# The expert stage of a routed vision-transformer layer, from chunks of 1024 rows against one weight set to chunks of two 512-row units side by side

## The chip, the cores and the metric

The kernel runs on one core of a Trainium2 chip. The metric is the device time of one execution in microseconds (us), here the median of three runs. Beside them stands one more execution, taken with the hardware profiler; all views of the profile are of that execution.

## The reference

Thirty-two images of 1024 patches each are embedded into 64 features. A single-head attention with layer norm follows, and then the part that matters here, a layer of 8 experts with top-1 routing:

```python
C = ceil(1.25 * T / E)                       # T = 32768 tokens, E = 8, C = 5120 slots per expert
idx = argmax(softmax(x @ gate_w + gate_b)); prb = its probability
pos = place of the token among those of its expert; kept = pos < C
hmid = relu(buf[e] @ w1[e] + b1[e])          # 64 -> 256
ybuf = hmid @ w2[e] + b2[e]                  # 256 -> 64
y = nan_to_num(ybuf[idx, pos] * (prb * kept), nan=0, posinf=1e4, neginf=-1e4)
out = layernorm(h + y)
```

All data are fp32. The output is 32 x 1024 rows of 64 numbers.

## The kernel before

The kernel has two stages that follow each other. The first runs over 32 windows, one image each: projections, attention, layer norm and gate, with the instructions of several images interleaved by hand (`run_windows`). GpSimd ends each window by scattering the 1024 rows into a DRAM tensor `slots` of 8 x 5120 rows by an indirect DMA each for 128 rows (L1052). A row has 66 numbers: 64 features, the probability and the token's number. None of this is touched by the change.

The second, the expert stage, begins when the last of those scatters has landed (the waits ahead of the first `load_chunk` on SyncE). It runs over 40 chunks of 1024 slots, 5 for each expert. Every engine has its own program, written out in order, and they meet only in semaphores. For chunk c:

- SyncE loads the chunk's rows into `b_in` (L368), a ring of 5 buffers (`NIN`). Each partition gets 8 rows that follow each other. The load for chunk c + 5 waits until chunk c has been normalized (`b_o_ready`). The weights of an expert have 2 buffers.
- TensorE turns the rows: 8 transposes into `p_st` (L546). Then come `hidden` (L555), which multiplies 65 rows (64 features and a row of ones that brings the bias) with `w1` in fp32, 4 products of 512 columns in 8 records, and the second product (L571): 16 products of 64 columns in 32 records, with the hidden values stationary and `w2` moving, so that the result already has tokens on partitions. It goes to one of two halves of `p_misc`. The order of the program is hidden(c), turn(c + 1), second product(c).
- ScalarE copies the turned rows out (`b_xT`, L664), applies Relu to the two halves of the hidden layer (L681, 1024 columns each), and computes squares and square root for the layer norm two chunks behind (L668, L672). In the first chunks this lag is one instead of two.
- VectorE adds `b2` (L908), makes three masks (L940, L941, L946) and replaces NaN, plus and minus infinity by three predicated copies (L927), multiplies by the probability (L932), adds the residual (L937), and normalizes (L944 to L971). The token numbers become integers in `b_ix` (L962). Before it writes `b_ix` and `b_o` of a ring place, it waits until the scatter that reads the place has landed. The steps of chunk c and of chunk c + 1 alternate in its program. For the first two chunks the tail of a chunk is issued at once, without the alternation (`if first and m < 2`).
- GpSimd waits for `b_o_ready` and issues 8 indirect DMAs of 128 rows, which scatter `b_o` to the output by `b_ix` (L1084).

Ahead of the stage TensorE runs 12 + 1 products that nobody reads (`keep_warm`). The loops are hardware loops over pairs of experts (`run_pairs`). A wait with a computed value goes through a register (`wait_apart`).

## Time and profile before

| | |
|---|---|
| Times of three runs | 1368.55, 1369.12, 1375.61 us |
| Median | 1369.12 us |
| The profiled execution | 1370.71 us |
| Its span in the profile | 1368.9 us, mean granted TensorE clock 0.933 of full speed |
| Busy: TensorE, VectorE, ScalarE, GpSimd | 1218.2, 941.1, 579.4, 884.0 us |
| First rows of the expert stage loaded from | 899.8 us |
| Output scatters (320) | 925.1 us to 1364.0 us |

A busy share is the mean over both stages, which have different limits, so the views that follow are cut to the expert stage. In all views PE is TensorE's products, PEld its weight loads, DVE VectorE, ACT ScalarE, POOL GpSimd and SP SyncE. L and a number is a line of the kernel. An fp32 product shows as two records, one of type fp32r as one. A granted clock of 1.00 is 2.4 GHz, one of 0.50 is 1.2 GHz.

### The profile page before, as it was taken

To read this page: it belongs to the slowest core of one execution; us is meant where nothing else is said; L and a number is where in the kernel's file an instruction comes from. 1 tells how busy PE (TensorE), PEld (TensorE's weight loads), DVE (VectorE), ACT (ScalarE), POOL (GpSimd) and SP (SyncE) were. 2 spreads that over 40 slices of the span, in tenths; PEclk is the share of its full clock that TensorE was granted. 3 is DMA by queue.
4 is the path that set the end of the run, shared out by engine and by line. 5 is a ranking of instruction groups with operands and counts; after the bars stand their busy time and mean duration, and the time that the engine had idled before them with its cause. 6 is when DMAs were issued, how large, how long until landed. Compare 5 with 4: busy or idle time off the path is not lost.

```text
span 1368.9 us, 21037 instructions
## 1 busy us (share of the span) xinstructions
PE 1218.2 (89%) x6088; PEld 770.6 (56%) x6088; DVE 941.1 (69%) x1766; ACT 579.4 (42%) x746; POOL 884.0 (65%) x950
## 2 busy tenths in 40 slices
PE   3999999999999999999999999599999999899600
PEld 2565666566565565656566555256667676666400
DVE  5577777777776777767777766329999777677610
ACT  1354455455554555545555544224444433333200
POOL 1137667657656666756766765737777777777776
PEclk9999999999999999999999999799999977969655
DMA  7843343333344234234334330011112111011000
GB/s 227 277 118 89 99 104 88 83 90 95 73 99 95 67 96 99 72 85 97 86 85 97 79 74 18 19 48 35 39 38 54 47 30 41 21 38 25 1 2 0
DMA packets 53485, 100.23 MB, mean 73 GB/s; under 512 B 22970, under 2 KB 25223, under 8 KB 53382
## 3 DMA queue, kind: packets, MB, share of 16 engines
q1 hardware_dynamic: 32646, 84.32, 24.9%
q0 software_dynamic: 20736, 14.62, 3.8%
q8 instruction: 54, 0.88, 0.3%
q14 instruction: 49, 0.40, 0.1%
HBM read 25.58 MB, written 38.34 MB: 47 GB/s over the span
## 4 chain that ended last, share of the span: by engine, by line
PE 66%; POOL 18%; issue 8%; DVE 3%; ACT 2%; DMA 2%; POOLq 1%; SPq 0%; DVEq 0%; ACTq 0%
PE p_u L478 17%; POOL out L1084 16%; PE p_st L462 10%; PE p_sm L448 9%; PE p_st L465 8%; PE p_misc L571 4%; PE p_misc L436 4%; PE p_misc L491 4%; PE p_misc L421 3%; PE p_sm L555 2%; PE p_u L555 2%; ACT b_h L681 1%; POOL slots L1052 1%; ACT pT L623 1%; DMA out<-b_o,b_ix 1%
## 5 line engine op out<-in xcount | busy, mean ns | idle before, releaser
L1052 POOL DMA_INDIRECT slots<-rows,idx x256 | 274.8, 1073 | 249.5 <-DVE acc L869 142.2
L782 DVE TENSOR_REDUCE mx<-p_sm 128x1 f32<-128x1024 f32 x252 | 308.3, 1224 | 166.9 <-PE p_sm L448 166.2
L1084 POOL DMA_INDIRECT out<-b_o,b_ix x320 | 341.7, 1068 | 119.9 <-issue 96.0
L623 ACT ACTIVATE pT<-p_st 128x1024 f32<-128x1024 f32 x256 | 262.3, 1024 | 266.7 <-PE p_st L465 265.3
L478 PE MATMUL p_u<-pT,vv 128*64 128x512 f32 x1024 | 261.8, 611 | 0.0
L462 PE MATMUL p_st<-mQ,sK 128*128 128x512 f32 x512 | 178.5, 430 | 6.4 <-ACT pT L623 3.9
L448 PE MATMUL p_sm<-sK,mQ 128*128 128x512 f32 x504 | 169.8, 418 | 4.5 <-DMA sK<-lo 3.5
L571 PE MATMUL p_misc<-b_w,b_h 128*128 128x64 f32 x1280 | 163.7, 290 | 10.3 <-ACT b_h L681 10.3
L571 PEld LDWEIGHTS p_misc<-b_w,b_h 128*128 128x128 f32 x1280 | 159.7, 206 | 19.7 <-ACT b_h L681 18.2
L465 PE MATMUL p_st<-mR,sR 72*128 72x512 f32 x512 | 161.0, 395 | 0.0
L462 PEld LDWEIGHTS p_st<-mQ,sK 128*128 128x128 f32 x512 | 83.6, 189 | 96.3 <-ACT pT L623 59.7
L448 PEld LDWEIGHTS p_sm<-sK,mQ 128*128 128x128 f32 x504 | 88.6, 191 | 70.4 <-DVE mx L782 28.1
L478 PEld LDWEIGHTS p_u<-pT,vv 128*64 128x64 f32 x1024 | 56.4, 135 | 106.5 <-issue 106.5
L465 PEld LDWEIGHTS p_st<-mR,sR 72*128 72x128 f32 x512 | 96.8, 189 | 23.6
L555 PE MATMUL p_sm<-b_xT,b_w 65*128 65x512 f32 x160 | 86.6, 668 | 9.8 <-ACT b_xT L664 9.0
L555 PE MATMUL p_u<-b_xT,b_w 65*128 65x512 f32 x160 | 88.6, 683 | 0.0
L927 DVE COPY_PREDICATED b_y<-b_m,b_big 128x512 f32<-128x512 uint8 x120 | 87.7, 731 | 0.5
L681 ACT ACTIVATE b_h<-p_sm 128x1024 f32<-128x1024 f32 x40 | 40.9, 1021 | 100.3 <-PE p_sm L555 100.3
L601 ACT ACTIVATE hi<-p_misc 128x1024 fp32r<-128x1024 f32 x32 | 32.8, 1024 | 115.8 <-PE p_misc L421 115.8
L436 PEld LDWEIGHTS p_misc<-w_px,xt 114*128 114x128 f32 x512 | 70.9, 194 | 5.8
L436 PE MATMUL p_misc<-w_px,xt 114*128 114x137 f32 x512 | 72.1, 284 | 0.0
L491 PEld LDWEIGHTS p_misc<-w_j,uu 128*128 128x128 f32 x512 | 62.0, 192 | 5.0 <-ACT uu L628 2.4
(146 smaller groups left out, 1543.6 us busy)
## 6 DMA issues: line engine op xcount, KB each, us to landing
mQ<-hi SPq DMA_DIRECT2D x64, 256.0 KB, 3.9
slots<-init POOLq DMA_DIRECT2D x16, 660.0 KB, 7.4
b_in<-slots SPq DMA_DIRECT2D x40, 264.0 KB, 2.7
sK<-hi SPq DMA_DIRECT2D x32, 256.0 KB, 5.0
sK<-lo SPq DMA_DIRECT2D x32, 256.0 KB, 4.5
mR<-lo SPq DMA_DIRECT2D x32, 256.0 KB, 3.9
sR<-hi SPq DMA_DIRECT2D x32, 256.0 KB, 4.5
out<-o SPq DMA_DIRECT2D x32, 256.0 KB, 4.2
```

The source lines that it names most:

```text
L436: last = pe.matmul(p_misc[:, j // 2, (j % 2) * GP:(j % 2 + 1) * GP], xt[0:KTOK, p, t * P:(t + 1) * P], w_px[:, :], start=True, stop=True)
L448: last = pe.matmul(max_place(n, j)[:, a, :], mQ[t][:, j * P:(j + 1) * P], sK[t][:, a * HALF:(a + 1) * HALF], start=True, stop=True)
L462: pe.matmul(p_st[:, a, :], sK[t][:, k * P:(k + 1) * P], mQ[t][:, a * HALF:(a + 1) * HALF], start=True, stop=False)
L465: last = pe.matmul(p_st[:, a, :], sR[p][0:D + NT, k * P:(k + 1) * P], mR[p][0:D + NT, a * HALF:(a + 1) * HALF], start=False, stop=True)
L478: last = pe.matmul(p_u[c:c + D, a, :], vv[:, p, k, :], pT[k % 4][:, a * HALF:(a + 1) * HALF], start=(r == 0), stop=(r == 3))
L491: last = pe.matmul(p_misc[:, j // 4, (j % 4) * GT:(j % 4 + 1) * GT], uu[:, j * P:(j + 1) * P], w_j[:, :], start=True, stop=True)
L555: last = pe.matmul((p_sm, p_u)[f][:, a, :], b_w1[:, q, f * P:(f + 1) * P], b_xT[0:KA, a * HALF:(a + 1) * HALF], start=True, stop=True)
L571: mm = pe.matmul(p_y[m % 2][:, j, :], b_h[:, f, j * P:(j + 1) * P], b_w2[:, q, f, :], start=(f == 0), stop=(f == HB - 1))
L623: act.activation(pT[k % 4][:, :], flat(p_st), ACT.Exp).then_inc(exp_done, 1)
L782: dve.tensor_reduce(mx[:, p, j:j + 1], flat(max_place(n, j)), AX.X, ALU.max).then_inc(max_done, 1)
L1052: pool.indirect_dma_start(slots, bass.IndirectOffsetOnAxis(ap=idx[:, p, j:j + 1], axis=0), rows[:, p, j, :], None, bounds_check=SLOTS - 1, ...
L1084: pool.indirect_dma_start(out_rows, bass.IndirectOffsetOnAxis(ap=b_ix[:, m % NIN, j:j + 1], axis=0), b_o[:, m % NIN, j, :], None, bounds_c ...
```

## The change

The 1024 rows of a chunk are taken as two units of 512, u = 0 and u = 1, that lie side by side on partitions: 64 features of each.

- SyncE loads each chunk three times: `b_in` as before, and each unit's 64 features into the half of `b_x` that is its own. The ring has 4 places. A reload waits for `b_c_ready`.
- TensorE turns both units with 4 transposes of 128 x 128. The first product is split in three fp32r products (high x high, low x high, high x low), each once for the upper and once for the lower 64 rows of the array: 12 products of 512 columns. In the second product `w2` is stationary (64 columns) and the hidden values move: 4 fp32 products of 512 columns, the units going to the upper and lower 64 partitions of one bank. The result has features on partitions, so 4 more transposes turn it back. The program's order is hidden(c), down(c - 1), rows_turn(c + 1), turn_back(c - 1).
- ScalarE rounds the turned rows to the high part (512 columns), adds `b1` inside the Relu and `b2` inside a copy of the sums. The order is Relu 0 of c, root of c - 3, Relu 1 of c, sums of c - 1, high part of c + 1, squares of c - 2. A Relu waits until down(c - 1) is done, since `b_h` has one buffer.
- VectorE makes the low part from the high one, splits each expert's `w1`, and multiplies by the probability straight from the turned-back sums. NaN and infinities are replaced after that multiplication, by three `tensor_scalar`, one addition and one predicated copy. Residual and layer norm are as before. The order in step c is: low part of c + 1, weighing of c - 1, sum of squares of c - 2, replacement of c - 1, output of c - 2, residual and centring of c - 1.
- GpSimd does the same 320 scatters. All loops are written out. The first chunks have no order of their own any more.

```diff
-NIN = 5
+NC = E * NCH
+NIN = 4
+UNIT = CH // 2
+UT = UNIT // P
...
+            def load_expert(e):
+                q = e % 2
+                for h in range(2):
+                    sp.dma_start(b_w1[h * D:(h + 1) * D, q, :], w1[e, :, :]).then_inc(e_loaded[q], 16)
+                sp.dma_start(b_w2[:, q, :], w2[e, :, :]).then_inc(e_loaded[q], 16)
+            def load_chunk(c):
+                r = c % NIN
+                sp.dma_start(b_in[:, r, :, :].rearrange("p (u j) w -> p u (j w)", u=2), slots_c[c, :, :, :])\
+                    .then_inc(c_loaded[r], 16)
+                for u in range(2):
+                    sp.dma_start(b_x[:, r, :, u * D:(u + 1) * D], slots_x[c, :, u, :, :]).then_inc(c_loaded[r], 16)
...
+            for c in range(NC):
+                if c + NIN < NC:
+                    sp.wait_ge(b_c_ready, c + 1)
+                    load_chunk(c + NIN)
+                e = c // NCH + 2
+                if c % NCH == NCH - 1 and e < E:
+                    sp.wait_ge(b_y_done, c + 1)
+                    load_expert(e)
...
+            def rows_turn(c):
+                r = c % NIN
+                pe.wait_ge(c_loaded[r], 48 * (c // NIN) + 48)
+                if c >= 2:
+                    pe.wait_ge(b_tl_ready, c - 1)
+                for j in range(UT):
+                    last = pe.transpose(p_st[:, c % 2, j * P:(j + 1) * P], b_x[:, r, j, :], c_id[:, :])
                 last.then_inc(b_t_done, 1)
+            def hidden(c):
+                q, i = c // NCH % 2, c % 2
+                pe.wait_ge(b_w_ready, c // NCH + 1)
+                pe.wait_ge(b_tl_ready, c + 1)
+                for f, out in ((0, p_sm), (1, p_u)):
+                    if c >= 1:
+                        pe.wait_ge(b_relu, HB * (c - 1) + f + 1)
+                    cols = slice(f * P, (f + 1) * P)
+                    for w, t in ((b_w1h, b_th[i]), (b_w1l, b_th[i]), (b_w1h, b_tl[i])):
+                        for u in range(2):
+                            h = slice(u * D, (u + 1) * D)
+                            last = pe.matmul(out[:, u, :], w[h, q, cols], t[h, :],
+                                             start=(w is b_w1h and t is b_th[i]), stop=(t is b_tl[i]))
+                    last.then_inc(b_h_done, 1)
+            def down(c):
+                q = c // NCH % 2
+                pe.wait_ge(b_relu, HB * c + HB)
+                if c >= 1:
+                    pe.wait_ge(b_yT_ready, c)
                 for f in range(HB):
+                    for u in range(2):
+                        last = pe.matmul(p_y[u * D:(u + 1) * D, :], b_w2[:, q, f * D:(f + 1) * D],
+                                         b_h[:, f, u, :], start=(f == 0), stop=(f == HB - 1))
+                last.then_inc(b_y_done, 1)
+            def turn_back(c):
+                pe.wait_ge(b_yT_ready, c + 1)
+                if c >= 1:
+                    pe.wait_ge(b_p_ready, c)
+                for j in range(UT):
+                    last = pe.transpose(p_misc[:, 1, j * P:(j + 1) * P], b_yT[:, j * P:(j + 1) * P], c_id[:, :])
+                last.then_inc(b_back_done, 1)
...
+            for c in range(NC + 1):
+                if c < NC:
+                    hidden(c)
+                if c >= 1:
+                    down(c - 1)
+                if c + 1 < NC:
+                    rows_turn(c + 1)
+                if c >= 1:
+                    turn_back(c - 1)
...
+            def columns_high(c):
                 act.wait_ge(b_t_done, c + 1)
+                if c >= 2:
+                    act.wait_ge(b_h_done, HB * (c - 1))
+                act.activation(b_th[c % 2][:, :], p_st[:, c % 2, :], ACT.Copy).then_inc(b_th_ready, 1)
+            def rectify(c, f):
+                q = c // NCH % 2
+                act.wait_ge(b_h_done, HB * c + f + 1)
+                if c >= 1:
+                    act.wait_ge(b_y_done, c)
+                act.activation(b_h[:, f, :, :].rearrange("p u t -> p (u t)"), flat((p_sm, p_u)[f]), ACT.Relu,
+                               bias=b_w2[:, q, HB * D + f:HB * D + f + 1]).then_inc(b_relu, 1)
+            def sums_copy(c):
+                q = c // NCH % 2
+                act.wait_ge(b_y_done, c + 1)
+                if c >= 1:
+                    act.wait_ge(b_back_done, c)
+                act.activation(b_yT[:, :], p_y, ACT.Identity, bias=b_w2[:, q, HB * D + HB:HB * D + HB + 1])\
+                    .then_inc(b_yT_ready, 1)
             def squares(c):
                 act.wait_ge(b_c_ready, c + 1)
+                if c >= 1:
+                    act.wait_ge(b_vs_ready, c)
+                act.activation(b_sq[:, :, :], b_c[c % 2][:, :, :], ACT.Square).then_inc(b_sq_ready, 1)
             def deviation(c):
                 act.wait_ge(b_vs_ready, c + 1)
+                if c >= 1:
+                    act.wait_ge(b_rs_ready, c)
                 act.activation(b_sd[:, :], b_vs[:, :], ACT.Sqrt, bias=b_eps[:, 0:1], scale=1.0 / D)\
                     .then_inc(b_sd_ready, 1)
...
+            columns_high(0)
+            for c in range(NC + 3):
+                if c < NC:
+                    rectify(c, 0)
+                if 0 <= c - 3:
+                    deviation(c - 3)
+                if c < NC:
+                    rectify(c, 1)
+                if 0 <= c - 1 < NC:
+                    sums_copy(c - 1)
+                if c + 1 < NC:
+                    columns_high(c + 1)
+                if 0 <= c - 2 < NC:
+                    squares(c - 2)
...
+            def split_expert(e):
+                q = e % 2
+                dve.wait_ge(e_loaded[q], 48 * (e // 2) + 48)
+                if e >= 2:
+                    dve.wait_ge(b_y_done, NCH * (e - 1))
+                link(dve.tensor_copy(b_w1h[:, q, :], b_w1[:, q, :]))
+                dve.tensor_tensor(b_w1l[:, q, :], b_w1[:, q, :], b_w1h[:, q, :].bitcast(F32), ALU.subtract)\
+                    .then_inc(b_w_ready, 1)
+            def columns_low(c):
+                i = c % 2
+                dve.wait_ge(b_th_ready, c + 1)
+                if c >= 2:
+                    dve.wait_ge(b_h_done, HB * (c - 1))
+                dve.tensor_tensor(b_tl[i][:, :], p_st[:, i, :], b_th[i][:, :].bitcast(F32), ALU.subtract)\
+                    .then_inc(b_tl_ready, 1)
+            def rows_in(c):
+                return b_in[:, c % NIN, :, :]
+            def weigh(c):
+                dve.wait_ge(b_back_done, c + 1)
+                if c >= 1:
+                    dve.wait_ge(b_num_ready, c)
+                dve.tensor_tensor(b_p[:, :, :].rearrange("p (u j) d -> p u j d", u=2), p_back,
+                                  per_token(rows_in(c)[:, :, D], D).rearrange("p (u j) d -> p u j d", u=2), ALU.mult)\
+                    .then_inc(b_p_ready, 1)
+            def sum_of_squares(c):
+                dve.wait_ge(b_sq_ready, c + 1)
+                if c >= 1:
+                    dve.wait_ge(b_sd_ready, c)
+                dve.tensor_reduce(b_vs[:, :], b_sq[:, :, :], AX.X, ALU.add).then_inc(b_vs_ready, 1)
+            def to_numbers(c):
+                dve.wait_ge(b_p_ready, c + 1)
+                if c >= 1:
+                    dve.wait_ge(b_u_ready, c)
+                dve.tensor_scalar(b_fin[:, :, :], b_p[:, :, :], 0.0, 0.0, ALU.mult, ALU.is_equal)
+                dve.tensor_scalar(b_pos[:, :, :], b_p[:, :, :], 0.0, 1e4, ALU.max, ALU.min)
+                dve.tensor_scalar(b_neg[:, :, :], b_p[:, :, :], 0.0, -1e4, ALU.min, ALU.max)\
+                    .then_inc(b_clip_ready, 1)
+                dve.wait_ge(b_clip_ready, c + 1)
+                dve.tensor_tensor(b_n[:, :, :], b_pos[:, :, :], b_neg[:, :, :], ALU.add).then_inc(b_n_ready, 1)
+                dve.wait_ge(b_n_ready, c + 1)
+                dve.copy_predicated(b_n[:, :, :], b_fin[:, :, :], b_p[:, :, :]).then_inc(b_num_ready, 1)
+            def normalized(c):
+                r = c % NIN
+                dve.wait_ge(b_sd_ready, c + 1)
+                dve.reciprocal(b_rs[:, :], b_sd[:, :]).then_inc(b_rs_ready, 1)
+                dve.wait_ge(b_rs_ready, c + 1)
+                if c >= NIN:
+                    dve.wait_ge(b_scattered[r], 16 * NT * (c // NIN))
+                dve.tensor_tensor(b_o[:, r, :, :], b_c[c % 2][:, :, :], per_token(b_rs[:, :], D), ALU.mult)
+                dve.tensor_copy(b_ix[:, r, :], b_id[:, c % 2, :]).then_inc(b_o_ready, 1)
+            def centred(c):
+                dve.wait_ge(b_num_ready, c + 1)
+                dve.tensor_tensor(b_u[:, :, :], b_n[:, :, :], rows_in(c)[:, :, 0:D], ALU.add)\
+                    .then_inc(b_u_ready, 1)
+                dve.wait_ge(b_u_ready, c + 1)
+                dve.tensor_reduce(b_mu[:, :], b_u[:, :, :], AX.X, ALU.add).then_inc(b_mu_ready, 1)
+                dve.tensor_copy(b_id[:, c % 2, :], rows_in(c)[:, :, D + 1])
+                dve.wait_ge(b_mu_ready, c + 1)
+                dve.tensor_scalar(b_mm[:, :], b_mu[:, :], 1.0 / D, None, ALU.mult).then_inc(b_mm_ready, 1)
+                dve.wait_ge(b_mm_ready, c + 1)
+                if c >= 2:
+                    dve.wait_ge(b_o_ready, c - 1)
+                dve.tensor_tensor(b_c[c % 2][:, :, :], b_u[:, :, :], per_token(b_mm[:, :], D), ALU.subtract)\
+                    .then_inc(b_c_ready, 1)
+            split_expert(0)
+            columns_low(0)
+            for c in range(NC + 2):
+                if c + 1 < NC:
+                    columns_low(c + 1)
+                if 0 <= c - 1 < NC:
+                    weigh(c - 1)
+                if 0 <= c - 2:
+                    sum_of_squares(c - 2)
+                if 0 <= c - 1 < NC:
+                    to_numbers(c - 1)
+                if c % NCH == 2 and c // NCH + 1 < E:
+                    split_expert(c // NCH + 1)
+                if 0 <= c - 2:
+                    normalized(c - 2)
+                if 0 <= c - 1 < NC:
+                    centred(c - 1)
...
```

## Rows read from the trace of the kernel before

**Rows 1.** Chain that ended last, by engine and line, 1000 us to the end.

```profile
by line: POOL out L1084 59.4%; issue 17.6%; PE p_misc L571 7.1%; PE p_u L555 3.3%; PE p_sm L555 2.9%; DMA out<-b_o,b_ix 2.1%; ACT b_h L681 2.0%; POOLq L1084 1.5%; DVE b_y L927 0.7%; DVE b_o L971 0.6%; POOLq L51 0.3%; DVE b_vs L964 0.2%; DVE
```

**Rows 2.** The page's groups: shapes, count, busy us, mean ns, idle before and its releasers.

```profile
L1084 POOL DMA_INDIRECT out<-b_o,b_ix x320 | 341.7, 1068 | 119.9 <-issue 96.0 <-DVE b_o L971 24.0
```

**Rows 3.** Line 1084: durations ns least/median/greatest, start of the first and the last.

```profile
L1084 POOL DMA_INDIRECT out<-b_o,b_ix x320: 971/973/1501, 925.1 to 1363.0; - x160
```

**Rows 4.** Waits of VectorE from 903 us on: total us, times, longest.

```profile
DVE b_ix L962 <- DMA out<-b_o,b_ix: 67.5, 22, 5.8
```

**Rows 5.** Timeline of TensorE, one chunk (start, us, records, idle before and releaser).

```profile
1061.15 3.79 PE L571 MATMUL p_misc<-b_w,b_h 128*128 128x64 f32 x32 [0.24 <-ACT b_h L681]
1064.77 1.94 PE L555 MATMUL p_sm<-b_xT,b_w 65*128 65x512 f32 x4
1068.26 1.04 PE L546 MATMUL p_st<-c_wide,b_in 128*64 128x128 f32 x8
```

**Rows 6.** The same in a later chunk, behind a pause of TensorE.

```profile
1212.26 3.60 PE L555 MATMUL p_sm<-b_xT,b_w 65*128 65x512 f32 x4 [0.83 <-ACT b_xT L664]
```

**Rows 7.** Windows: busy us (records) by engine, then PEclk, DMA share, GB/s.

```profile
924.00:1092.00 168.00, 161.77 (x959) 117.16 (x958) 153.93 (x307) 74.31 (x97) 130.30 (x121) 1.00 0.17 43
1092.00:1290.00 198.00, 184.97 (x854) 129.21 (x852) 141.87 (x288) 67.51 (x89) 154.44 (x144) 0.79 0.12 27
```

**Rows 8.** Timeline of TensorE in the attention stage: column halves, then fp32r products.

```profile
508.11 1.94 PE L478 MATMUL p_u<-pT,vv 128*64 128x512 f32 x8
...
510.37 0.71 PE L421 MATMUL p_misc<-xh,w_qkh 114*128 114x512 f32 x2
...
511.86 0.63 PE L462 MATMUL p_st<-mQ,sK 128*128 128x512 f32 x2
```

**Rows 9.** Groups by shape of VectorE and ScalarE, 903 us on, columns as rows 2.

```profile
L927 DVE COPY_PREDICATED b_y<-b_m,b_big 128x512 f32<-128x512 uint8 x120 | 87.7, 731 | 0.5
...
L681 ACT ACTIVATE b_h<-p_sm 128x1024 f32<-128x1024 f32 x40 | 40.9, 1021 | 100.3 <-PE p_sm L555 100.3
...
L971 DVE TENSOR_TENSOR b_o<-b_c,b_rs 128x512 f32<-128x512 f32 x40 | 28.0, 701 | 2.8
L908 DVE TENSOR_TENSOR b_y<-p_misc,b_b 128x512 f32<-128x512 f32 x40 | 27.5, 687 | 32.1 <-PE p_misc L571 30.1 <-issue 1.9
...
L940 DVE TENSOR_SCALAR b_m<-b_y 128x512 uint8<-128x512 f32 x40 | 17.0, 424 | 0.1
...
L672 ACT ACTIVATE b_sd<-b_vs,b_eps 128x8 f32<-128x8 f32 x40 | 11.8, 295 | 60.1 <-DVE b_vs L964 60.1
L949 DVE TENSOR_SCALAR b_mm<-b_mu 128x8 f32<-128x8 f32 x40 | 9.6, 240 | 0.1
...
L969 DVE RECIPROCAL b_rs<-b_sd 128x8 f32<-128x8 f32 x40 | 7.6, 190 | 1.7 <-ACT b_sd L672 1.7
```

**Rows 10.** Timeline at the start of the expert stage, SyncE and TensorE.

```profile
899.76 2.23 SPq L368 DMA_DIRECT2D b_in<-slots  x5
...
902.52 1.06 PE L546 MATMUL p_st<-c_wide,b_in 128*64 128x128 f32 x8 [2.22 <-DMA b_in<-slots]
```

**Rows 11.** Timeline: first square root, first output, first scatter.

```profile
921.69 1.28 ACT L672 ACT_TABLE_LOAD   x1
...
923.55 0.69 DVE L971 TENSOR_TENSOR b_o<-b_c,b_rs 128x512 f32<-128x512 f32 x1
...
925.14 1.11 POOL L1084 DMA_INDIRECT out<-b_o,b_ix  x1 [22.75 <-DVE b_o L971]
```

**Rows 12.** Timeline: two scatters beside VectorE.

```profile
1114.82 0.68 DVE L964 TENSOR_REDUCE b_vs<-b_sq 128x8 f32<-128x512 f32 x1
1115.11 0.97 POOL L1084 DMA_INDIRECT out<-b_o,b_ix  x1 [0.30 <-issue]
...
1116.33 0.69 DVE L971 TENSOR_TENSOR b_o<-b_c,b_rs 128x512 f32<-128x512 f32 x1
1116.39 1.48 POOL L1084 DMA_INDIRECT out<-b_o,b_ix  x1 [0.30 <-issue]
```

239 lines of the change are left out of this document (51 added, 188 removed).

## The prediction

> **What bounds the kernel now.** I read the chain of waits first, because the two stages have different limits and a busy share over both says little. From 1000 us to the end, which lies wholly in the expert stage, the chain is made of output scatters and the "issue" gaps between them [rows 1]. The reader is to see there that TensorE's products come in only in the first 50 us. The group of the scatters gives the price: 320 of 1.068 us each, 341.7 us, with 96.0 us of gaps of 0.30 us [rows 2]. The first starts at 925.1 us and the last at 1363.0 us [rows 3]. So GpSimd runs without a pause for 438.9 us, or 8 x 1.368 = 10.94 us for a chunk. The waits of VectorE say the same from the other side: 67.5 us for scatters to land, in order to get a ring place back [rows 4]. TensorE needs 1.77 + 1.71 + 1.28 + 3.62 = 8.4 us for a chunk at full clock, the distance between the starts of its pieces [rows 5], so it runs ahead until the ring is full.
>
> **The sum's frame.** The profiled execution took 1370.71 us, its span is 1368.9, so 1.8 us lie outside; it stands 1.6 us above the median of 1369.12. The last scatter ends at 1364.0, 4.9 us before the span's end. A change in this stage can move the time by three things only: when the first scatter starts, what a scatter costs, and whether a chunk is ready every 10.94 us.
>
> **The scatter itself** isn't changed. Its least duration is 0.971 us and its mean 1.068 [rows 2, 3]; the rest is 0.097 x 320 = 31 us. The timeline shows what makes it. A scatter that starts in the middle of a reduction takes 0.97. One that starts at 1116.39, 0.06 us into the output multiplication, takes 1.48, and what it has in excess is about what was left of that instruction [rows 12]. I take it that a scatter waits for VectorE instructions with two SBUF inputs, and for the fast `tensor_scalar` (0.42 us for 512 elements, where an addition takes 0.69) [rows 9]. Per chunk there were 5 of the first kind, 3 predicated copies of 0.73 and 2 `tensor_scalar`; now there are 4, 1 and 3. If the excess goes by the square of their durations, it falls from 4.3 to 3.0 units, or 31 us to about 22: a gain of 9 us. Bounds: 31 us of gain, none, or 10 us of loss, if the phases meet badly.
>
> The Trainium skill has this rule in "SBUF — State Buffer", "Who interferes with whom": the second port pair of VectorE is shared with GpSimd and held for a whole instruction by operations with two SBUF inputs or in a two-port mode. By it the gain is real as far as those instructions become fewer, and the trace agrees with its 1.48 against 0.97.
>
> **The work of a chunk now, first on TensorE.**
> - Hidden: 12 fp32r products of 512 columns. Six of them one after the other took 1.49 us (510.37 to 511.86) [rows 8], so 3.0 us if the two units exclude each other, 1.5 if they run fully side by side. What is nearest is the pair of column halves in the attention stage: 8 fp32 records in 1.9 us [rows 8], where 4 records of the same width take 1.77 in a row [rows 5]; about 0.24 instead of 0.44 each. I take 1.8.
> - Down: 4 fp32 products, 8 records, of exactly that form: 1.94 us; 3.5 if in a row.
> - Eight transposes of 128 x 128: 8 of half the width took 1.04 [rows 5], so 0.5 to 1.1 for each group of 4; I take 0.7. They lie beside ScalarE's work.
>
> TensorE thus falls from 8.4 to about 5.2 us at 2.4 GHz. By itself that is worth nothing, since it waited already.
>
> "TensorEngine Tiling", "Key Properties", in the Trainium skill says that tiles run in parallel and that a change of the tiling mode drains the engine. Hidden, down and the transposes are three modes. No row here shows row tiles; the column halves agree with the first part. By that part alone hidden would take 1.5 us and a chunk 9.0; for the drains neither the page nor a row has a price.
>
> **The loop.** The new orders close a ring through four engines. hidden(c + 1) needs the low part of c + 1, which VectorE makes only after centring c - 2. That stands behind output(c - 3), which waits for the root on ScalarE. The root is queued behind Relu 0 of c, and this Relu waits for down(c - 1), behind hidden(c) on TensorE. So in each chunk these follow each other with nothing beside them:
> - low part of the next chunk 0.69, as the addition that reads 512 elements from PSUM [rows 9], and 0.08 to TensorE;
> - hidden and down 1.8 + 1.94 = 3.74;
> - Relu 1.02 and root 0.30 [rows 9], 0.09 for two hand-overs;
> - reciprocal 0.19, output 0.61, numbers to `b_ix` 0.20, 0.04 of hand-over;
> - residual 0.68, row sum 0.68 [rows 12], scaling 0.24, centring 0.60, three hand-overs of 0.04: 2.32.
>
> Sum: 0.77 + 3.74 + 1.41 + 1.04 + 2.32 = 9.28 us. Weighing, replacement (3 x 0.42, 0.69, 0.73) and the sum of squares, 4.0 us, lie beside hidden, down, Relu and root, 5.1 us; the split of `w1`, 0.6 us on every fifth chunk, fits in barely. Behind the Relu's added wait stand the sums copy and the high part, and for them wait turn_back and VectorE.
>
> 9.28 us would still be under 10.94. But TensorE now works in one burst of 3.7 us and two small groups of transposes, and pauses for 4 us in each chunk, five times the 0.83 us behind which it fell to 1.2 GHz. At 1.2 GHz hidden and down take 7.5 us, and they lie on the ring: 13.0 us for a chunk. At that pace TensorE is mostly busy and should rise again, as it did in rows 7's second window. There the mean of 0.79 means 0.42 of the time at the lower clock, with TensorE busy in 185 of 198 us. With more pauses I take 0.6: 9.28 + 0.6 x 3.74 = 11.5 us. The bounds are 9.3 and 13.0.
>
> **The start.** The first chunk's order of its own is gone. Before, from the first load issue at 899.76 [rows 10] to the first scatter at 925.14 [rows 11] there were 25.4 us. Now the load is three pieces, two of them in runs of 256 bytes: 904.5 instead of 902.5 (one load took 2.7 us, the added pieces cost 0.5 to 4; I take 2). Turn, high and low part 0.7 + 0.6 + 0.7: 906.5. The low part of chunk 1 follows hidden, two Relus and a high part: 911. From there to the low parts of chunks 2 and 3 it is 3.74 + 2 x 1.02 + 0.6 + 0.6 + 0.7 + 0.3 = 8.0 us each: 927. Then hidden(3) and down(2) 3.74, Relu 1.02, table load 1.28 [rows 11], root 0.30, output 1.1: 934.5. At 1.2 GHz throughout some 13 us more, 948. I take 941. The first scatter starts 0.9 us after its rows, as before (923.55 + 0.69 to 925.14) [rows 11].
>
> **The loads.** 40 x 3 instead of 40, issued four chunks ahead; at 11 us a chunk a landing of 5 or even 10 us is hidden. The ring of 4 instead of 5 holds 4 x 10.94 = 44 us of scatters. It costs nothing while VectorE is at most three chunks ahead. Without that cover each scatter's landing would be on the chain. The second load of weights now waits for down; it has five chunks of time. Written-out loops: nothing, bounds -1 to +2.
>
> **The sum.** 941 + 39 x 11.53 (449.7) + 0.9 + the last 8 scatters, beside an idle VectorE, 9.9 + 4.9 + 1.8 = 1408 us, 38 above the profiled execution.
>
> **Rivals.**
> - The scatters stay the bound. If the clock holds, or 9.3 us are right nearly throughout: 934.5 + 0.9 + 438.9 - 9 + 4.9 + 1.8 = 1372 us. For it speaks the margin of 1.6 us per chunk and the full clock up to 1092 us; against it the pauses. 0.24.
> - Always 1.2 GHz, or row tiles that exclude each other (which gives 10.5 us and 15.5 us): 948 + 39 x 13.0 + 17.5 = 1473 us. For it: 4 us of pause. Against: the clock came back several times between 1092 and 1290. 0.13.
> - Faster: fewer instructions on VectorE give GpSimd its 0.97 us, at 10.2 us a chunk. This decides if the ring runs below 10.2 us and less than half of the 31 us stays. 934.5 + 0.9 + 438.9 - 31 + 6.7 = 1350, with half of it 1366; middle 1358. For it: two predicated copies fewer. Against: four two-input operations stay and the start loses 9 us. 0.13.
>
> **How the numbers follow.** The forecast has 0.50, with a range of its own of 1384 to 1440 (0.4 to 0.8 of the time at the lower clock, or other starts). The range for 8 in 10 takes in the scatter-bound case and stops inside the two outer ones: 1363 to 1464. 0.5% is 6.8 us, so faster is below 1362.3 and slower above 1376.0; this is about what a measurement of this kernel can tell. The scatter-bound case divides into 0.03 faster, 0.14 same and 0.07 slower, the faster rival into 0.12 and 0.01 same. So faster is 0.15, same 0.15, slower 0.07 + 0.50 + 0.13 = 0.70.
>
> **What would show it.** The first output scatter at 935 to 948 us. Scatters with pauses in front of them put down to VectorE's output, over 100 us in all, where they were 1.3 besides the first. A distance of 11 to 12 us between the Relus of successive chunks. A granted clock near 0.7 in the stage, with hidden taking 1.8 us in some chunks and 3.6 in others. A mean scatter of 1.00 to 1.05 us. VectorE waiting for the root, no longer for scatters to land. It is wrong if GpSimd's pauses stay under 5 us, if hidden takes 3 us at full clock, or if the clock is 1.00 in spite of the pauses.

## The result: slower by 1.6%, and the profile after

The changed kernel took 1395.1 us in the median of four runs (1390.5 to 1398.0), the kernel before 1369.7 beside it. The ratio is 1.0159, with an interval of 1.0124 to 1.0193. The profiled execution took 1398.0, span 1396.2. Forecast were 1408 and "slower"; the mechanism behind that number was not the one that came.

First the page's row of the output scatters, their line, and the waits from 903 us on (us, times, longest), which answer to [rows 2], [rows 3] and [rows 4].

```profile
L1130 POOL DMA_INDIRECT out<-b_o,b_ix x320 | 350.4, 1095 | 136.9 <-issue 93.0
...
L1130 POOL DMA_INDIRECT out<-b_o,b_ix x320: 970/974/1507, 944.6 to 1392.3; - x160
...
DVE b_rs L992 <- ACT b_sd L725: 98.6, 38, 4.6
POOL out L1130 <- issue: 93.0, 305, 0.3
POOL out L1130 <- DVE b_ix L997: 44.0, 15, 38.7
DVE b_o L996 <- DMA out<-b_o,b_ix: 14.5, 6, 5.5
```

VectorE now waits for the root, 98.6 us, as forecast. But GpSimd waited for rows only 44.0 - 38.7 = 5.3 us besides the first time, where the forecast names over 100 as its sign. So the scatters still set the pace, and they became dearer: 1095 ns in place of 1068. The end is the first scatter's start, the scatters, the gaps between them, pauses, and what follows the last:

| us | start | scatters | gaps | pauses | tail | span |
|---|---|---|---|---|---|---|
| before | 925.1 | 341.7 | 96.0 | 1.3 | 4.9 | 1368.9 |
| after | 944.6 | 350.4 | 93.0 | 5.3 | 2.9 | 1396.2 |
| difference | +19.5 | +8.7 | -3.0 | +4.0 | -2.0 | +27.3 |

The first load was issued 3.5 us later than before. The way from there to the first scatter is 15.9 us longer, which is the largest part of the loss.

The windows (columns as in [rows 7]) show the clock: lower at once, where it had been 1.00 to 1092 us. The third and fourth are two pieces of one round of 10.24 us.

```profile
945.00:1030.00 85.00, 52.23 (x226) 27.46 (x224) 61.44 (x131) 32.02 (x48) 65.71 (x61) 0.79 0.25 54
1030.00:1230.00 200.00, 118.72 (x546) 65.53 (x548) 151.87 (x324) 76.70 (x115) 158.21 (x138) 0.83 0.29 66
...
1041.50:1044.90 3.40, 2.96 (x14) 2.07 (x16) 3.37 (x7) 0.40 (x1) 2.68 (x3) 0.50 0.68 155
1044.90:1051.80 6.90, 3.13 (x16) 1.26 (x16) 4.92 (x13) 3.66 (x6) 5.48 (x5) 0.99 0.02 1
```

The timeline of one chunk, with only the rows on the ring and the scatters beside them, shows both the ring and why a scatter is dear.

```profile
1037.66 0.29 ACT L725 ACTIVATE b_sd<-b_vs,b_eps 128x8 f32<-128x8 f32 x1
...
1037.93 0.97 POOL L1130 DMA_INDIRECT out<-b_o,b_ix  x1 [0.31 <-issue]
...
1038.90 0.68 DVE L1001 TENSOR_TENSOR b_u<-b_n,b_in 128x512 f32<-128x512 f32 x1
1039.21 1.22 POOL L1130 DMA_INDIRECT out<-b_o,b_ix  x1 [0.30 <-DVE b_ix L997]
...
1040.55 0.69 DVE L1011 TENSOR_TENSOR b_c<-b_u,b_mm 128x512 f32<-128x512 f32 x1
1040.74 1.35 POOL L1130 DMA_INDIRECT out<-b_o,b_ix  x1 [0.30 <-issue]
1041.16 0.68 DVE L955 TENSOR_TENSOR b_tl<-p_st,b_th 128x512 fp32r<-128x512 f32 x1
...
1041.94 0.80 PE L576 MATMUL p_sm<-b_th,b_w1h 64*128 64x512 f32 x2 [1.69 <-issue]
...
1042.36 0.67 DVE L973 TENSOR_REDUCE b_vs<-b_sq 128x8 f32<-128x512 f32 x1
1042.39 0.98 POOL L1130 DMA_INDIRECT out<-b_o,b_ix  x1 [0.30 <-issue]
...
1044.21 0.66 PE L576 MATMUL p_u<-b_tl,b_w1h 64*128 64x512 f32 x2
...
1044.80 1.98 PE L588 MATMUL p_misc<-b_h,b_w 128*64 128x512 f32 x8
1045.05 0.74 DVE L987 COPY_PREDICATED b_n<-b_fin,b_p 128x512 f32<-128x512 uint8 x1
1045.10 1.50 POOL L1130 DMA_INDIRECT out<-b_o,b_ix  x1 [0.30 <-issue]
...
1046.89 1.11 ACT L704 ACTIVATE b_h<-p_sm,b_w 128x1024 f32<-128x1024 f32 x1 [4.99 <-PE p_misc L588]
...
1047.90 0.29 ACT L725 ACTIVATE b_sd<-b_vs,b_eps 128x8 f32<-128x8 f32 x1
```

The ring. From root to root 10.24 us: 3.50 to the low part, 0.78 to hidden, 2.86 to down, 2.09 to Relu 0, 1.01 to the root. From 1030 to 1222 us each round is a copy of the last, to 0.02 us (roots at 1037.66, 1047.90, 1058.14, 1068.38). The pairs of hidden stand 0.43 us apart, and it is 2.86 us until down starts; down takes 1.98. In each chunk hidden thus runs at 1.2 GHz, behind a pause of 1.69 us, and down at 2.4: the granted clock is 0.50 from 1041.5 to 1044.9 us, while hidden runs, and 0.99 in the rest of the round.

The scatter. It waits for the VectorE instruction with two SBUF inputs, or the fast `tensor_scalar`, that runs already when it starts; what it has in excess is all that is left of it 0.12 us after the scatter's start. Copy at 1045.05: 1045.05 + 0.74 - 1045.10 - 0.12 = 0.57 left, 1.50 - 0.97 = 0.53 in excess. Centring: 0.38 left, 0.38 in excess. Residual: 0.25 and 0.25. Beside the reduction, that reads one tensor, 0.98. This is [rows 12] again. The Trainium skill, "SBUF — State Buffer", "Who interferes with whom", lets a two-input operation contend with a GpSimd instruction that reads SBUF, and `tensor_reduce` never; the trace agrees with 1.50 and 1.35 against 0.98. Of the 39.7 us in excess, added up scatter by scatter, the predicated copy has 14.8 (36 scatters), centring 9.3, residual 6.7, the `tensor_scalar` of line 981 3.5. Operations that read one tensor in PSUM (L955, L965) and reductions have next to none.

An instruction that begins together with the scatter does not delay it, which [rows 12] alone would not tell. In the trace of the kernel before:

```profile
1083.48 0.97 POOL L1084 DMA_INDIRECT out<-b_o,b_ix  x1 [0.30 <-issue]
1083.49 0.72 DVE L971 TENSOR_TENSOR b_o<-b_c,b_rs 128x512 f32<-128x512 f32 x1
```

This is the output again, which delayed its scatter by 0.51 us in [rows 12], where it had begun 0.06 us before it. In the kernel before 45 instructions of these two kinds began between 0.02 us before a scatter's start and 0.12 us behind it, and none of them delayed it. Of the 141 that had begun earlier, 138 did.

The two together. 10.24 us hold exactly seven scatters with their gaps, and the eighth of each chunk stays over. So for some 210 us the same seven places come back in each round, and four of them are bad ones: 0.25 + 0.38 + 0.15 (at 1043.68, beside line 981) + 0.53 = 1.31 us for seven scatters, a mean of 0.971 + 0.187 = 1.158. Measured were 1.161 from 1060 to 1160 us, against 1.039 from 1260 to 1360, where VectorE waits for landings and eight scatters fit in a round. Spread evenly over 10.24 us, the six long instructions and the two fast ones would give an excess of about 0.11 in place of 0.187; that is an estimate from their durations and the 0.12 us. The 147 scatters of the rounds from 1007 to 1222 us hold 27.6 of the 39.7 us.

The start, in the timeline:

```profile
903.30 0.38 SPq L380 DMA_DIRECT2D b_in<-slots  x1
...
908.02 0.80 PE L561 MATMUL p_st<-c_wide,b_x 128*128 128x128 f32 x4 [4.39 <-DMA b_x<-slots]
...
944.62 1.07 POOL L1130 DMA_INDIRECT out<-b_o,b_ix  x1 [38.70 <-DVE b_ix L997]
```

From the first load issue to the first scatter 41.3 us, where [rows 10, 11] have 25.4. The issue itself is 3.5 us later. It stood anywhere from 899.8 to 904.0 in the traces of the table below, with and without the change, so these 3.5 us are not put down to the change.

### The profile page after: what moved, and what is told of

It is laid out like the page before. It is cut to its first block, busy times and chain, and to the rows that moved or that the text cites. A ratio compares the mean times of both kernels' runs of the same rounds, so it can differ in the third digit from the quotient of the medians.

```text
span 1396.2 us, 19236 instructions
## 1 busy us (share of the span) xinstructions
PE 1109.0 (79%) x5288; PEld 646.6 (46%) x5288; DVE 932.5 (67%) x1778; ACT 587.6 (42%) x786; POOL 889.8 (64%) x950
## 4 chain that ended last, share of the span: by engine, by line
PE 67%; POOL 13%; issue 11%; ACT 5%; DVE 2%; DMA 1%; SPq 0%; POOLq 0%; ACTq 0%; DVEq 0%
PE p_u L491 16%; POOL out L1130 11%; PE p_st L475 10%; PE p_sm L461 9%; PE p_st L478 8%; PE p_misc L449 4%; PE p_misc L588 4%; PE p_misc L504 4%; PE p_sm L576 3%; PE p_misc L434 3%; PE p_u L576 2%; ACT b_h L704 2%; PE p_misc L597 1%; POOL slots L1098 1%; ACT b_yT L712 1%
## 5 line engine op out<-in xcount | busy, mean ns | idle before, releaser
L1130 POOL DMA_INDIRECT out<-b_o,b_ix x320 | 350.4, 1095 | 136.9 <-issue 93.0
L1098 POOL DMA_INDIRECT slots<-rows,idx x256 | 271.3, 1060 | 253.8 <-DVE acc L910 171.7
L655 ACT ACTIVATE pT<-p_st 128x1024 f32<-128x1024 f32 x256 | 262.2, 1024 | 269.1 <-PE p_st L478 264.5
L704 ACT ACTIVATE b_h<-p_sm,b_w 128x1024 f32<-128x1024 f32 x40 | 44.6, 1114 | 208.5 <-PE p_misc L588 205.9
L597 PE MATMUL p_misc<-c_wide,b_yT 128*128 128x128 f32 x160 | 28.4, 304 | 99.1 <-ACT b_yT L712 99.1
L588 PE MATMUL p_misc<-b_h,b_w 128*64 128x512 f32 x320 | 90.2, 690 | 0.0
L633 ACT ACTIVATE hi<-p_misc 128x1024 fp32r<-128x1024 f32 x32 | 32.8, 1024 | 118.6 <-PE p_misc L434 118.6
L576 PE MATMUL p_sm<-b_th,b_w1h 64*128 64x512 f32 x80 | 30.8, 752 | 64.1 <-issue 61.7
L992 DVE RECIPROCAL b_rs<-b_sd 128x8 f32<-128x8 f32 x40 | 8.1, 202 | 98.6 <-ACT b_sd L725 98.6
L597 PEld LDWEIGHTS p_misc<-c_wide,b_yT 128*128 128x128 f32 x160 | 18.2, 149 | 109.9 <-ACT b_yT L712 109.9
```

The costliest lines, as they stand in the source:

```text
L576: last = pe.matmul(out[:, u, :], w[h, q, cols], t[h, :], start=(w is b_w1h and t is b_th[i]), stop=(t is b_tl[i]))
L588: last = pe.matmul(p_y[u * D:(u + 1) * D, :], b_w2[:, q, f * D:(f + 1) * D], b_h[:, f, u, :], start=(f == 0), stop=(f == HB - 1))
L655: act.activation(pT[k % 4][:, :], flat(p_st), ACT.Exp).then_inc(exp_done, 1)
L1098: pool.indirect_dma_start(slots, bass.IndirectOffsetOnAxis(ap=idx[:, p, j:j + 1], axis=0), rows[:, p, j, :], None, bounds_check=SLOTS - 1, ...
L1130: pool.indirect_dma_start(out_rows, bass.IndirectOffsetOnAxis(ap=b_ix[:, r, j:j + 1], axis=0), b_o[:, r, j, :], None, bounds_check=T - 1, ...
```

## The experiments

Median and ratio are from all runs, the ratio to the kernel before on the same chip with its interval; the other columns are from the profiled execution. The changed kernel itself was not run again on the chips of the experiments, where the kernel before took 1373.4 and 1373.9 us. So its ratio, and not its time, is what the others are held against. "Excess" is the scatters' busy time above 320 x 0.971; "pauses" leave out the wait for the first rows.

| kernel | median us | ratio | start | excess | pauses |
|---|---|---|---|---|---|
| before | 1369.7 | | 925.1 | 31.0 | 1.3 |
| after | 1395.1 | 1.0159 (1.0124 to 1.0193) | 944.6 | 39.7 | 5.3 |
| root_early | 1374.9 | 1.0010 (0.9982 to 1.0038) | 940.0 | 26.9 | 1.0 |
| fill_pauses | 1384.3 | 1.0076 (1.0049 to 1.0103) | 941.3 | 30.8 | 2.2 |
| out_ring2 | 1394.0 | 1.0135 (1.0095 to 1.0174) | 941.1 | 32.9 | 4.7 |
| no_replace | 1372.6 | 0.9987 (0.9959 to 1.0014) | 940.6 | 7.2 | 12.7 |
| root_no_replace | 1359.8 | 0.9885 (0.9834 to 0.9936) | 935.5 | 11.3 | 0.9 |
| root_first_b | 1378.9 | 1.0017 (0.9981 to 1.0054) | 930.0 | 27.5 | 7.6 |
| root_psum_first_b | 1363.3 | 0.9924 (0.9899 to 0.9949) | 928.4 | 15.1 | 7.7 |
| before_no_replace_b | 1372.0 | 0.9981 (0.9954 to 1.0008) | 926.9 | 27.7 | 2.9 |

**The ring opened (root_early).** The root moves from behind the next Relu to behind its own squares.

```diff
                 if c < NC:
                     rectify(c, 0)
-                if 0 <= c - 3:
-                    deviation(c - 3)
...
                     squares(c - 2)
+                    deviation(c - 2)
```

> The square root of chunk c - 2 is issued right behind its squares, instead of behind Relu 0 of the next chunk but one; nothing else is changed. Theory of the ring (root, output and centring wait for down of the next chunk): the distance between two chunks in the free stretch falls from 10.24 us to 8.5 to 9.6, VectorE's 98.6 us of waits for the root fall under 20, and the first output scatter comes 4 to 8 us earlier (936 to 941). As the scatters set the end, the time falls only by that start: 1386 to 1392. Rival (the ring sets the pace of the stage): the time falls by more than 15 us.

```profile
DVE b_o L995 <- DMA out<-b_o,b_ix: 91.0, 28, 5.5
...
DVE b_rs L991 <- ACT b_sd L725: 0.4, 1, 0.4
```

Against after the span is 18.4 us shorter: 4.6 at the start, 12.8 in the scatters, 4.3 in pauses, less 3.3 in gaps. VectorE waits for landings again, as in [rows 4], and no longer for the root. I had expected 1386 to 1392 us, the start alone; the fall of 20 us was the rival's, but not by its cause. The larger part came from cheaper scatters, not from pauses. From 940 to 1050 us the mean scatter was 1.115 here too, and from 1060 to 1260 it was 1.044. With rounds of 7.6 to 9.3 us the output ring was full after some 110 us, where the changed kernel needed 280. So the lock between ring and scatters was costly even though the ring was the faster of the two, and what root_early changed was above all how long the dear stretch lasts.

**The clock kept up (fill_pauses).** Four products that nobody reads are put into TensorE's pauses; the ring stays closed.

```diff
                 if c + 1 < NC:
                     rows_turn(c + 1)
+                    for _ in range(2):
+                        pe.matmul(p_st[:, c % 2, :], c_id[:, :], pT[0][:, 0:HALF], start=True, stop=True)
                 if c >= 1:
                     turn_back(c - 1)
+                if c + 1 < NC:
+                    pe.wait_ge(b_relu, HB * c + 1)
+                    for _ in range(2):
+                        pe.matmul(p_sm[:, 0, :], c_id[:, :], pT[0][:, 0:HALF], start=True, stop=True)
```

> Four fp32 products per chunk that nobody reads are added in TensorE's pauses (two behind rows_turn into the free half of p_st, two ahead of hidden into p_sm), so that the pauses shrink below 1 us. Theory that the clock only matters in front of the scatters' bound: the granted clock in the stage rises from 0.81 to over 0.95, hidden takes 1.4 us in place of 2.8, the free distance of chunks falls to 9 us, and the time changes by the start alone, -2 to -6 us. Rival (the clock was worth 0.3 us and more in each chunk): 15 us or more less. If the added products delay hidden, the free distance stays above 10 us and the time is the same.

```profile
1030.00:1230.00 200.00, 158.91 (x680) 72.57 (x678) 144.86 (x310) 76.16 (x115) 155.51 (x147) 0.98 0.28 63
```

```profile
1043.59 0.50 PE L576 MATMUL p_sm<-b_th,b_w1h 64*128 64x512 f32 x2
...
1044.83 0.41 PE L576 MATMUL p_u<-b_tl,b_w1h 64*128 64x512 f32 x2
1045.17 1.94 PE L588 MATMUL p_misc<-b_h,b_w 128*64 128x512 f32 x8
```

The clock is 0.98 in place of 0.83, the pairs stand 0.23 us apart, and hidden gives down its turn after 1.58 us in place of 2.86. The free ring has 8.92 us (roots at 1030.38, 1039.31, 1048.23, 1057.17), 1.32 less, of which hidden is 1.28. The ring at full clock is thus even shorter than the forecast's 9.28. Spans: 13.3 us below after, 8.9 of it in the scatters, where I had expected a gain of 2 to 6 us from the start alone. From 960 to 1060 us, in rounds of 8.93 us with six scatters, the mean scatter was 1.189, with the same four delays as in the changed kernel. From 1060 to 1160 it was 1.046. Most of those rounds are steady too, 10.8 us with eight scatters, but hold three delays only, of 0.25, 0.15 and 0.19 us. So a lock can be dear or cheap. The dear one belongs to the stretch in which VectorE runs ahead, whatever the length of the round, and the better clock ended it sooner.

**The output ring cut to two (out_ring2).** `b_o`, `b_ix` and `b_scattered` get two places instead of four, so that landings hold VectorE back.

```diff
+NO = 2
...
-                r = c % NIN
+                r = c % NO
```

> The ring of output rows and indices has 2 places instead of 4; the ring of loads keeps 4. Theory of the lock step (while VectorE runs ahead at 10.24 us per chunk, seven scatters fall into each round at the same places beside VectorE, and 1.16 us each is the result; once the ring is full the mean is 1.02 to 1.08): with two places the free stretch ends some 100 us earlier, the mean of all scatters falls from 1.095 to 1.05 to 1.07, and the time falls by 5 to 14 us. Rival (a smaller ring lets GpSimd starve): over 5 us of pauses more, the time the same or longer by 5 to 15 us.

The scatters became 6.8 us cheaper, a mean of 1.074, but the root is still waited for, 108.6 us, and the median is where it was; the 5 to 14 us that I had expected did not come. The gaps took back 3.2 us and the tail 5.3: the last scatter starts at 1384.6 and the span ends 8.2 us behind its end, where all others here have 2.9 or 4.9. No record shows what was waited for there; this stays open.

**The replacement of NaN and infinities left out (no_replace, and with the root early root_no_replace).** The residual reads `b_p` directly.

```diff
             def to_numbers(c):
-                dve.tensor_scalar(b_fin[:, :, :], b_p[:, :, :], 0.0, 0.0, ALU.mult, ALU.is_equal)
...
-                dve.copy_predicated(b_n[:, :, :], b_fin[:, :, :], b_p[:, :, :]).then_inc(b_num_ready, 1)
...
-                dve.tensor_tensor(b_u[:, :, :], b_n[:, :, :], rows_in(c)[:, :, 0:D], ALU.add)\
+                dve.tensor_tensor(b_u[:, :, :], b_p[:, :, :], rows_in(c)[:, :, 0:D], ALU.add)\
```

> Leaves out the replacement of NaN and infinities: three tensor_scalar, one addition and one predicated copy less per chunk. Theory that scatters wait for VectorE instructions with two SBUF inputs or in the fast mode: 20.4 of the 39 us of excess lie on these five, so the mean scatter falls from 1.095 to 1.03 to 1.06 and the time by 10 to 22 us with the start (the first scatter 2 to 4 us earlier). Rival (the excess comes from DMA traffic of the 256-byte loads or from descriptor work): mean 1.09 or more, time the same but for the start.

> root_early, which leaves out the replacement of NaN and infinities. no_replace alone had a mean scatter of 0.993 us but 12.7 us of pauses besides the first, since the ring (10.3 us a chunk, 204 us of waits for the root) had become slower than eight scatters (10.3 us). Theory of the ring: with the root issued early the pauses fall under 3 us, the mean scatter stays at 0.98 to 1.01, and the time is 8 to 16 us under no_replace: ratio to the kernel before 0.985 to 0.993. Rival (the pauses come from loads or landings): pauses of 8 us or more stay.

no_replace first, then root_no_replace:

```profile
DVE b_rs L984 <- ACT b_sd L725: 203.7, 40, 6.9
POOL out L1122 <- issue: 96.5, 308, 1.6
POOL out L1122 <- DVE b_ix L989: 48.0, 12, 35.3
```

```profile
DVE b_rs L983 <- ACT b_sd L725: 15.3, 33, 0.5
...
POOL out L1121 <- DVE b_ix L988: 31.4, 4, 30.5
```

The excess fell from 39.7 to 7.2 us, with the loads and the scatters as they were; so it came neither from the loads of 256 bytes nor from the scatter's own work. With scatters of 0.993 + 0.30 us a chunk needs 10.3, and the ring, 10.3 us in most rounds and 10.7 in the mean, becomes the bound: 12.7 us of pauses. With the root early they are 0.9. Of the 13.0 us between the two spans the pauses are 11.8 and the start 5.1, less 4.1 in the scatters. So the ring is real and has the price that its rows give; in the changed kernel it lay just below the scatters' 11.2 us.

**The same left out of the kernel before (before_no_replace_b).** Three masks and three predicated copies go, six of the instructions that a scatter can meet. A wait on `b_y_read` is added ahead of the weighing.

```diff
-                    dve.tensor_scalar(b_m[:, 0, :, :], ny, FMAX, None, ALU.is_gt)
-                    dve.tensor_scalar(b_m[:, 1, :, :], ny, -FMAX, None, ALU.is_lt)
...
-                    one_at = replace(0, masks_at)
```

> before_no_replace again, on a chip where the kernel before takes its usual time. The kernel before, which leaves out the replacement of NaN and infinities. Theory that its scatters too wait for VectorE: mean scatter 1.00 (1.001 in its first trace), first scatter 3 to 4 us earlier, time 20 to 27 us less than the kernel before, ratio 0.980 to 0.986. Rival (VectorE's work is hidden there): 0.995 or more.

```profile
1103.95 0.69 DVE L962 TENSOR_TENSOR b_o<-b_c,b_rs 128x512 f32<-128x512 f32 x1
1104.15 1.34 POOL L1075 DMA_INDIRECT out<-b_o,b_ix  x1 [0.30 <-issue]
...
1105.76 0.68 DVE L938 TENSOR_TENSOR b_u<-b_p,b_in 128x512 f32<-128x512 f32 x1
1105.80 1.50 POOL L1075 DMA_INDIRECT out<-b_o,b_ix  x1 [0.30 <-issue]
```

The time stayed, where I had expected 20 to 27 us less, and the excess fell from 31.0 to 27.7 only. What is left concentrates on residual (10.8), output (8.6) and centring (7.4): VectorE is released by a landing, 112.7 us of such waits, and then runs the same instructions into the next scatters' starts, in chunk after chunk. Fewer bad instructions do not mean fewer meetings.

**Row tiles in another order (units_apart).** All products of one unit ahead of the other's.

```diff
-                    for w, t in ((b_w1h, b_th[i]), (b_w1l, b_th[i]), (b_w1h, b_tl[i])):
-                        for u in range(2):
+                    for u in range(2):
+                        for w, t in ((b_w1h, b_th[i]), (b_w1l, b_th[i]), (b_w1h, b_tl[i])):
```

> The changed kernel with the order of hidden's products turned round: the three products of unit 0, then the three of unit 1, for each half, instead of the units by turns. Theory that by turns they run side by side on two row halves (a pair in 0.23 us at 2.4 GHz and 0.43 at 1.2), and that one half alone takes as long for one product: hidden goes from 2.8 to about 5 us at 1.2 GHz (1.4 to 2.6 at 2.4), the ring from 10.24 to 11.6 to 12.7 us, GpSimd pauses 20 to 60 us, time 1410 to 1455. Rival (products of two halves overlap in any order, or did not overlap at all): hidden and time unchanged.

```profile
992.84 0.80 PE L576 MATMUL p_sm<-b_th,b_w1h 64*128 64x512 f32 x2 [1.24 <-issue]
993.40 0.67 PE L576 MATMUL p_sm<-b_th,b_w1l 64*128 64x512 f32 x2
...
995.11 0.67 PE L576 MATMUL p_u<-b_tl,b_w1h 64*128 64x512 f32 x2
```

The steps are 0.43 us, as after: hidden takes 2.87 us at 1.2 GHz, 2.86 in the other order. I had expected it longer. The halves overlap although one unit's three products stand ahead of the other's in the kernel's text; what brought them side by side the trace does not show.

This kernel and the next three ran on a chip on which the kernel before took 1493 us. In their traces ScalarE's Relus were held for 126 to 169 us by what the trace names only "remote". The medians were 1430.2 us for units_apart, 1450.3 for root_first, 1473.6 for root_psum_first and 1508.3 for before_no_replace, with ratios of 0.954, 0.962, 0.985 and 1.009. So the changed kernel's variants were ahead there, the first by 4.6% (0.943 to 0.965), and which of the two designs is faster hung on the chip. Why is open: no trace of the kernel before was taken there. These times are not used below, and three of the kernels were run again, on a chip as the others' (the runs with _b).

**The first chunk ahead, and the replacement in PSUM (root_first, root_psum_first).** root_first is root_early with squares, root, sum and output of chunk 0 issued one round earlier, right behind its centring, and the root's table loaded ahead. root_psum_first adds weighing in place in PSUM, and `tensor_scalar` and copy that read PSUM, all of the reference still computed.

```diff
+                if c == 1:
+                    squares(0)
+                    deviation(0)
...
-                dve.tensor_tensor(b_p[:, :, :].rearrange("p (u j) d -> p u j d", u=2), p_back,
+                dve.tensor_tensor(p_back, p_back,
...
-                dve.copy_predicated(b_n[:, :, :], b_fin[:, :, :], b_p[:, :, :]).then_inc(b_num_ready, 1)
+                dve.copy_predicated(turned_order(b_n), turned_order(b_fin), p_flat).then_inc(b_num_ready, 1)
```

> As root_early, and the tail of chunk 0 is finished inside its own round on ScalarE and VectorE (squares, root, sum, output right behind its centring), and a root that nobody uses is computed ahead of the stage, so that the table is loaded there. Theory that the late start is paid one for one, because the scatters set the end: first scatter 5 to 8 us earlier than root_early's 940.0, time 1367 to 1371. Rival (chunk 1 then comes late and GpSimd pauses for what was gained): the same first scatter, but 4 us or more of pauses and 1373 to 1377.

> As root_first, and the weighted sums stay in PSUM, in place of the turned-back sums; the masks and clips read them there, one addition becomes part of a clip that reads PSUM and SBUF, and the predicated copy takes its data from PSUM. VectorE instructions with two SBUF inputs or in the fast mode fall from 8 to 4 or 5 per chunk, and it has about 0.8 us more work. Theory of the shared read port: the scatters' excess falls from 26 us to 12 to 20 and the time to 1356 to 1364. Rival (what counts is how long VectorE works, or the phase alone): excess 25 us or more, time as root_first or longer.

> The kernel before, which leaves out the replacement of NaN and infinities (three masks, three predicated copies). Theory that its scatters wait for VectorE in the same way: mean scatter from 1.068 to 1.00 to 1.04, first scatter 3 to 4 us earlier, time 1344 to 1360. It also prices this part for the kernel before: if the gain is as large as the 22 us of the changed kernel without it, the replacement in one predicated copy was no gain over that in three. Rival (VectorE's work is hidden in the kernel before): 1364 or more.

> root_first again, on a chip where the kernel before takes its usual time. As root_early (first scatter at 940.0 us, 1374.9 us), with the tail of chunk 0 finished in its own round and the table loaded ahead of the stage. Theory that the start is paid one for one: first scatter 932 to 936 us, time 5 to 8 us under root_early's, 0.990 to 1.000 of the kernel before. Rival (chunk 1 comes late): pauses of 4 us or more, ratio 1.000 to 1.004.

> root_psum_first again, on a chip where the kernel before takes its usual time. The weighted sums stay in PSUM and fewer VectorE instructions have two SBUF inputs. Its first trace had a mean scatter of 1.021 us. Theory of the shared read port: mean scatter 1.01 to 1.04 here too, time 8 to 14 us under root_first's, ratio to the kernel before 0.982 to 0.992. Rival (its longer VectorE round sets the pace instead): pauses of 8 us or more and no gain over root_first.

root_first_b begins 10 us before root_early and gains little or nothing by it: chunk 1 comes late, with 6.6 us of pauses more, and the ratios are the same within their intervals. An earlier start thus pays only if the chunks behind it come earlier too. root_psum_first_b is the fastest that computes everything:

```profile
L1145 POOL DMA_INDIRECT out<-b_o,b_ix x320 | 325.8, 1018 | 129.4 <-issue 95.7
```

Against root_first_b 12.4 of the 13.6 us are in the scatters. The two `tensor_scalar` that now read PSUM were running already at 36 starts of scatters and delayed none; the one that reads SBUF (L995) was at 8, and delayed all of them. The copy, which now reads its data from PSUM, met 8 starts and delayed none, where in the changed kernel it met 36 for 14.8 us. Six of the 8 had begun with the scatter, so they tell nothing. In the two others it had been running for 0.4 us and still had 0.2 to delay. One of them:

```profile
1034.38 0.73 DVE L997 COPY_PREDICATED b_n<-b_fin,p_misc 128x512 f32<-128x512 uint8 x1
...
1034.77 0.97 POOL L1145 DMA_INDIRECT out<-b_o,b_ix  x1 [0.30 <-issue]
```

What is left is the output's, 7.1 us in 32 meetings, and centring's, 3.0. On the other chip the mean scatter was 1.018 for the same kernel, as here, but 1.004 for before_no_replace, where _b has 1.057. It is the same kernel with another timing, 146 us of pauses in place of 2.9: the meetings hang on it.

## Why the prediction came out near, step by step

- **The frame** (start, scatter, readiness) served: the terms of the table add up to the span by the way they are made, and each term could be held against the forecast's.
- **Hidden, down, turns.** Hidden 1.58 us until down starts at full clock (1.8 taken), down 1.98 (1.94), four transposes 0.66 (0.7). The row tiles do not exclude each other.
- **The ring** exists with the forecast's members and was 8.92 us at full clock (9.28 forecast). **The failed step is the one that makes 11.5 of it: "9.28 + 0.6 x 3.74".** The lower clock meets hidden only, since down already runs at 2.4 GHz: 1.28 us in place of 2.2, and with the shorter ring 10.24 in place of 11.5. The 0.6 was carried over from a stretch with other pauses; here the lower clock had a third of the round. At 10.24 the ring stays below the scatters' 11.2, and the pauses are 5.3 us. The sign "over 100 us" was wrong by the forecast's own sum as well: 11.53 us against eight scatters of 1.04 + 0.30 leaves 0.8 us a chunk, some 30 in all. The text's limit was 5 us, so the measured 5.3 speak for the rival "the scatters stay the bound", and so does the distance of the chunks, 10.24 and not 11 to 12.
- **The scatter.** Forecast a gain of 9 us, measured a loss of 8.7, inside the bounds but of the wrong sign. The rule of which instructions delay it was right. What was missing in it is that the operation has to run already when the scatter starts. The failed assumption was that meetings are spread evenly, so that the excess goes by the squares of the durations. They are locked: seven starts per round at fixed places.
- **The start.** 41.3 us from first load issue to first scatter, 42.1 forecast (941 + 0.9 - 899.8). The 2 us taken for the added loads had no row; from the first issue to the first product it was 4.7 us (903.30 to 908.02), as forecast (904.5 less 899.8).
- **The sum.** The rival of 1372 plus 9.2 (first scatter at 944.6, it had 935.4), 17.7 (scatters at +8.7 in place of -9), 4.0, -3.0 and -2.0 gives 1397.9, measured 1398.0. The forecast had 36 us more than that rival, 30 for a slow ring and 6.5 for the start; a later start and dear scatters gave nearly as much. The nearness of 1408 is in good part chance.

Shown by undoing: ring and lock (root_early, root_no_replace), clock (fill_pauses), the share of copy and `tensor_scalar` (root_psum_first_b). Not shown: why the start could be taken back only in part, and why the phases settle where they do. For the second there is an argument: by the rule above a delayed scatter ends at a time that VectorE sets, whatever its own start was, so each delay ties the scatters behind it to VectorE's round. No run tests it.

## What to carry to other kernels

Where GpSimd issues indirect DMAs back to back, a two-input VectorE operation in SBUF costs time by where it stands, and not only by how many there are: look in the timeline what runs at each start, and let such operations read PSUM. A loop through several engines that is faster than the bound is not free, since its steady round can fix bad meetings for as long as it runs ahead. Price a lower clock for each product by what TensorE did just before it, not as a share of time over all of them.

## What the runs showed of the hardware

- A scatter of 128 rows takes 0.97 us and 0.30 to the next. It waits for the rest of a two-input or fast VectorE operation in SBUF that already runs when it starts, less 0.12 us. One that begins between 0.02 us before it and 0.12 us behind it delays nothing (45 cases in the kernel before, none delayed). The predicated copy counts as one with its data in SBUF (36 meetings, 14.8 us). With them in PSUM it delayed none, but only two meetings of root_psum_first_b can tell, and three of root_psum_first; the `tensor_scalar` that read PSUM delayed none of 36.
- Two halves of the rows of TensorE overlap at 0.23 us a pair (2.4 GHz) and 0.43 (1.2 GHz), the latter in either order of the kernel's text. "TensorEngine Tiling (Array Packing)", "Key Properties", in the Trainium skill says that tiles run in parallel; these numbers agree. Its drain at a change of mode can't be seen here: with three modes in a chunk down still took 1.98 us.
- TensorE ran at 1.2 GHz in hidden and at 2.4 in down of the same burst, in chunk after chunk, with two pauses, of 2.46 and 1.69 us, in each (granted clock 0.50 from 1041.5 to 1044.9 us, 0.99 from there to 1051.8).
